# Variance of the gates in the PSUM bank, Newton's step for x on GpSimd

## What is computed

```python
x = x + conv_ref(ln_c(x), Wk, bk, Wq, bq, Wv, bv, Wr, br, heads=8)
#   k = relu(Wk x + bk), q = relu(Wq x + bq), v = Wv x + bv
#   context = k v^T per head (8 x 8), attended = context^T q, out = Wr attended + br
t = to_tokens(x)
t = t + ffn_ref(ln_t(t), router_w, router_b, expert_w, expert_b)
#   p = softmax(t router_w + router_b); the two best experts, their weights made to sum to 1
#   out = sum over the two of weight * (t expert_w[e] + expert_b[e])
x = from_tokens(t, x)
# both norms: (v - mean) / sqrt(var + eps) over the 64 channels, eps 1e-6 and 1e-5
```

## Time and profile before

| | |
|---|---|
| median of 3 runs | 662.58 us (661.94 to 663.03) |
| profiled execution, its time | 661.13 us |
| profiled execution, its span | 659.3 us |
| mean granted TensorE clock | 0.991 |
| busy: TensorE | 612.2 us (93%) |
| busy: VectorE | 506.5 us (77%) |
| busy: ScalarE | 420.3 us (64%) |
| busy: GpSimd | 396.4 us (60%) |
| chain that ended last, by engine | TensorE 72%, VectorE 18%, issue 6% |

### The profile page before, as it was taken

The page is one execution under the profiler, slowest core; times in us unless marked ns, Lnnn a source line. Parts: engine busy times, 40 slices in busy tenths (PEclk is TensorE's granted clock), DMA queues, the critical chain, the costliest instruction groups (busy, mean ns, idle before and its releaser), DMA issues.

```text
span 659.3 us, 21452 instructions
## 1 busy us (share of the span) xinstructions
PE 612.2 (93%) x8318; PEld 277.4 (42%) x8318; DVE 506.5 (77%) x1176; ACT 420.3 (64%) x800; POOL 396.4 (60%) x350
## 2 busy tenths in 40 slices
PE   3799989779999999999999999999999999999997
PEld 1566656444444444444444444444333333332232
DVE  3434444798888888898888888988798999989954
ACT  2265646576767676766676676775857667676552
POOL 7223252127666566667666566656677767777986
PEclk9999989799999999999999999999999999999999
DMA  6132535395555566655556665544565667545652
GB/s 151 33 100 67 146 100 130 81 226 132 139 131 138 141 158 160 145 134 127 145 129 147 146 162 129 129 120 109 133 150 135 145 159 176 130 96 120 151 132 49
DMA packets 32663, 86.22 MB, mean 131 GB/s; under 512 B 7650, under 2 KB 7826, under 8 KB 32562
## 3 DMA queue, kind: packets, MB, share of 16 engines
q1 hardware_dynamic: 32082, 84.64, 53.4%
q0 software_dynamic: 288, 0.19, 0.2%
q10 hardware_dynamic: 192, 0.01, 0.0%
HBM read 34.47 MB, written 16.78 MB: 78 GB/s over the span
## 4 chain that ended last, share of the span: by engine, by line
PE 72%; DVE 18%; issue 6%; ACT 2%; POOL 2%; DVEq 0%; ACTq 0%; POOLq 0%
PE bank L1103 28%; PE bank L1089 8%; PE bank L1026 6%; PE bank L1004 5%; PE bank L990 5%; DVE z L834 4%; PE bank L949 3%; PE bank L973 3%; PE bank L1050 3%; PE bank L1100 3%; DVE x L734 2%; DVE osb L844 2%; PE bank L1075 2%; DVE xnT L689 2%; DVE bank L749 1%
## 5 line engine op out<-in xcount | busy, mean ns | idle before, releaser
L442 POOL TENSOR_TENSOR z<-gbs,x1d 128x512 f32<-128x512 f32 x256 | 320.6, 1278 | 170.8 <-ACT gbs L579 78.0
L1106 PE MATMUL bank<-z,ew 128*64 128x512 f32 x512 | 244.6, 599 | 0.0
L1103 PE MATMUL bank<-z,ew 128*64 128x512 f32 x512 | 243.6, 598 | 0.0
L579 ACT COPY gbs<-bank 128x512 f32<-128x512 f32 x256 | 140.9, 595 | 46.4 <-PE bank L1089 46.0
L834 DVE TENSOR_TENSOR z<-bank,x1d 128x512 f32<-128x512 f32 x256 | 165.3, 678 | 6.3 <-PE bank L1089 6.3
L433 POOL TENSOR_TENSOR xsq<-xin 128x512 f32<-128x512 f32 x64 | 65.4, 1044 | 85.0 <-DMA xin<-in_x_dram 67.4
L1103 PEld LDWEIGHTS bank<-z,ew 128*64 128x64 f32 x512 | 64.9, 136 | 103.4 <-issue 96.9
L1089 PE MATMUL bank<-grows,sel 64*64 64x512 f16 x1024 | 85.7, 387 | 6.1 <-ACT grows L573 4.8
L503 ACT COPY xn<-bank 128x512 f32<-128x512 f32 x64 | 34.4, 590 | 62.4 <-PE bank L949 62.4
L1106 PEld LDWEIGHTS bank<-z,ew 128*64 128x64 f32 x512 | 64.4, 136 | 1.1 <-POOL z L442 1.1
L734 DVE SCALAR_TENSOR_TENSOR x<-bank,br_col,x_again 128x512 f32<-128x512 f32 x64 | 45.0, 745 | 20.0 <-PE bank L1050 20.0
(11 more groups left out here) (135 smaller groups left out, 819.9 us busy)
## 6 DMA issues: line engine op xcount, KB each, us to landing
x1d<-x SPq DMA_DIRECT2D x128, 256.0 KB, 4.5
xin<-in_x_dram SPq DMA_DIRECT2D x64, 256.0 KB, 4.2
x_again<-in_x_dram SPq DMA_DIRECT2D x64, 256.0 KB, 4.1
out_dram<-osb SPq DMA_DIRECT2D x128, 128.0 KB, 2.6
k<-in_const_dram SPq DMA_DIRECT2D x1, 453.5 KB, 4.0
ew_nat<-in_L_ffn_expert_w_dram POOLq DMA_DIRECT2D x2, 64.0 KB, 6.4
sel<-in_const_sel_dram SPq DMA_DIRECT2D x1, 128.0 KB, 3.3
bk_rows<-bk_wide ACTq DMA_DIRECT2D x6, 1.0 KB, 1.7
```

Source lines behind the costliest of these rows:

```text
L442: pool.tensor_tensor(z[:, 1, i % R_Z, :], gbs[:, i % R_Z, :], x1d[:, g % 2, 1, u * NT:(u + 1) * NT], ALU.mult).then_inc(z_pool, 1)
L579: nc.scalar.copy(gbs[:, i % R_Z, :], bank[:, :]).then_inc(taken_of(("spread", i, 1)), 1)
L1103: pe.matmul(out_bank[0:C, :], ew[:, j, :], z[:, 0, i % R_Z, :], start=False, stop=(j == PAIRS - 1), skip_group_check=True).then_inc(prod_d ...
L1106: pe.matmul(out_bank[C:P, :], ew[:, j, :], z[:, 1, i % R_Z, :], start=False, stop=(j == PAIRS - 1), skip_group_check=True).then_inc(prod_d ...
```

## The change

Two edits. In the gates the variance is kept in a third short row of bank 7 (`dev_work[2]`) and no longer in SBUF (`bstat[:, 1]`); the first of Newton's three products multiplies it with the root (one operand in PSUM, one in SBUF) where it multiplied the root with itself (both in SBUF), and the second multiplies that with the root. And Newton's step for x leaves VectorE: GpSimd makes it in four instructions of 128x16, `x_newton`, ahead of its products of slot 3; `normalise` and the next group's `x_deviations` wait for the new semaphore `xstat_pool`.

```diff
@@ sizes and banks
-        dev_work = [bank[7][:, QG * E + QG * i:QG * E + QG * (i + 1)] for i in range(2)]
+        dev_work = [bank[7][:, QG * E + QG * i:QG * E + QG * (i + 1)] for i in range(3)]
+        xstat_pool = sem("xstat_pool")
-        N_XSTAT, N_GATE = 7, 27
+        N_XSTAT, N_NEWTON, N_GATE = 4, 4, 27
@@ GpSimd
+            def x_newton(g):
+
+                own, root, work = g * N_NEWTON, xstat[:, 4, :], xstat[:, 5, :]
+                pool.wait_ge(xstat_root, g + 1)
+                pool.tensor_tensor(work, root, root, ALU.mult).then_inc(xstat_pool, 1)
+                pool.wait_ge(xstat_pool, own + 1)
+                pool.tensor_tensor(work, work, xstat[:, 2, :], ALU.mult).then_inc(xstat_pool, 1)
+                pool.wait_ge(xstat_pool, own + 2)
+                pool.tensor_scalar(work, work, -0.5, 1.5, ALU.mult, ALU.add).then_inc(xstat_pool, 1)
+                pool.wait_ge(xstat_pool, own + 3)
+                pool.tensor_tensor(rstd[:, g % 2].rearrange("p u a -> p (u a)"), work, root, ALU.mult
+                                   ).then_inc(xstat_pool, 1)
...
             for n in range(STEPS):
                 for k in range(SLOTS):
+                    if k == 3 and real(n - L_COLS):
+                        x_newton(n - L_COLS)
                     for i in iterations(n, k + 1):
                         product(i)
@@ VectorE, x_deviations and normalise
-                    lambda: dve.reciprocal(xstat[:, 3, :], xstat[:, 2, :]),
-                    *newton(rstd[:, g % 2].rearrange("p u a -> p (u a)"), xstat[:, 4, :], xstat[:, 2, :],
-                            (xstat[:, 5, :], xstat[:, 0, :]))]
+                    lambda: dve.reciprocal(xstat[:, 3, :], xstat[:, 2, :])]
...
-                    elif k == 4:
-                        dve.wait_ge(xstat_root, g + 1)
+                        upto(dve, xstat_pool, g * N_NEWTON)
...
-                dve.wait_ge(xstat_dve, (g + 1) * N_XSTAT)
+                dve.wait_ge(xstat_pool, (g + 1) * N_NEWTON)
@@ VectorE, gates
+                def gate_root():
+                    dve.wait_ge(dev_root, p + 1)
+                    return dve.scalar_tensor_tensor(dev_work[0], dev_work[2], -0.5, bstat[:, 3, :], ALU.mult, ALU.mult)
...
-                    lambda: dve.tensor_scalar(bstat[:, 1, :], dev_work[1], 0.0, EPS_FFN, ALU.max, ALU.add),
-                    lambda: dve.reciprocal(bstat[:, 2, :], bstat[:, 1, :]),
-                    rooted, dev[1], dev[2],
+                    lambda: dve.tensor_scalar(dev_work[2], dev_work[1], 0.0, EPS_FFN, ALU.max, ALU.add),
+                    lambda: dve.reciprocal(bstat[:, 2, :], dev_work[2]),
+                    gate_root,
+                    lambda: dve.tensor_tensor(dev_work[1], dev_work[0], bstat[:, 3, :], ALU.mult),
+                    lambda: dve.scalar_tensor_tensor(bstat[:, 0, :], dev_work[1], 1.5, bstat[:, 3, :],
+                                                     ALU.add, ALU.mult),
@@ VectorE, the loop over steps and slots
-                    if k == 3 and real(n - L_COLS):
-                        x_deviations(n - L_COLS, 4, N_XSTAT)
```

More of the change, by code:

```diff
@@ L651, in then @@
                     dve.wait_ge(set_dve, n_set[0])
[L653 to L657, removed]
             def halves(a):
@@ L749, in start @@
                     return dve.scalar_tensor_tensor(halves(dev_work[0]), mean, -1.0, mean, ALU.mult, ALU.mult)
-                def rooted():
-                    dve.wait_ge(dev_root, p + 1)
-                    return dev[0]()
                 def choose():
@@ L789, in total @@
                     return dve.tensor_scalar(second_work, gstat[:, 4, :], 1.0, None, ALU.add)
-                dev = newton(bstat[:, 0, :], bstat[:, 3, :], bstat[:, 1, :], dev_work)
                 steps = [
```

## The result

| | before | with the change |
|---|---|---|
| median of the runs | 662.26 us (660.6 to 663.03, 4 runs) | 654.08 us (650.39 to 654.75, 4 runs) |
| profiled execution, its time | 661.13 us | 654.75 us |
| profiled execution, its span | 659.3 us | 652.9 us |
| mean granted clock | 0.991 | 0.994 |

The ratio is 0.9868, with a 95% interval from 0.9827 to 0.991. The forecast was 652.8 us, a gain of 9.8. The medians differ by 8.2 us, the two profiled executions by 6.4.

What follows compares the result with a forecast made beforehand. TensorE was taken as the bound from 144 to 444 us, losing time only to VectorE's lateness. 7.75 + 1.9 + 0.15 = 9.8 us off the 662.58 us median gave 652.8 us, range 649.8 to 658.0.

Steps and rivals of the forecast that it cites:

- What bounds the kernel: From 144 to 444 us TensorE is the bound; VectorE's lateness for L834 costs it 1.55 us in one loaded step.
- Gates' variance in the bank: Gates' L655 falls to 0.20 us, but the stall moves to L767: gain 0.55 us of VectorE's time, not 0.97.
- The price of 0.065 us: 62 cycles more for a PSUM source, in two gates' instructions; by it the ramp gains 0.26 us less, sum 9.5.
- 0.55 and 1.52 us of VectorE's time: Loaded step: 0.55 from the gates' edit and 1.52 from Newton's step leaving VectorE bring L834 2.07 us earlier.
- The sum of the loaded steps: From 144 to 444 us the full 1.55 us comes back in five loaded steps: 7.75 us.
- The ramp, 1.9 us: From 115 to 146 us, Newton's step leaving three VectorE chains saves 0.5 + 0.9 + 0.5 = 1.9 us.
- Newton's step on GpSimd, 1.3 us, hidden: Four dependent 16-column instructions take 1.3 us, hidden from 144 us on where GpSimd idled 1.65 us between products.
- Rival A: L767 waits behind GpSimd's whole Newton chain, so 1.0 of each 1.55 us stays lost: 4.7 us gained, 657.9; chance 0.19.
- Before 115 us nothing: In early steps Newton's step has 1.91 us and uses 1.3, so TensorE neither gains nor loses.
- B: Newton's step on GpSimd late in eight early steps, losing 8 x (T - 1.9); at T = 3.6 us, 666.4; chance 0.06.
- C: Nothing measurable, within 1.3 us: another lateness, say ScalarE's exponential, replaces VectorE's at the same place; chance 0.08.
- D: More than the sum: the ramp's shorter wait for keys keeps the clock up, 2.6 us more, 650.2; chance 0.07.

Runs made afterwards that it cites:

- the mended order: GpSimd's ten set-up instructions for the experts' bias placed ahead of Newton's step in step 11, against the changed kernel: 653.68 us; again on another chip 652.55 us.
- both orders mended: Changed kernel with GpSimd's expert-bias set-up ahead of Newton's step in step 11 and VectorE's x variance in slot 1 behind the gates: 651.6 us, ratio 0.985.
- the kernels with more work: Changed kernel with GpSimd's four Newton instructions for x made two or three times over: 658.86 us (ratio 0.995) and 671.95 us (ratio 1.0152).
- the third group: Runs on one chip beside the kernel before (661.69 us): x's variance behind the gates 656.11, both repairs 651.6, expert-bias set-up ahead again 652.55 us.

## Why the prediction was right, and where its sizes were off

*What bounds the kernel.* Right: TensorE had one large wait for VectorE in five loaded steps, and without it the stretch from turn_x to the experts takes 2.72 us, as in the steps with a fold.

*Gates' variance in the bank.* Right in its mechanism: L792 takes 0.185 to 0.20 us everywhere, and the stall moved to L770 (0.70 us in place of 0.44), as forecast. The price of 0.065 us for an operand read from the bank did not show: the reciprocal of 128x32 takes 0.357 us from the bank and took 0.353 from SBUF, and L792 is no longer than an unstalled L655. Only the weight of the edits was misjudged: the prediction added 0.55 and 1.52 us of VectorE's time and did not price one alone. Its own numbers do that for x: 0.55 us later with 0.4 to spare is 0.15 lost in the stretch, and the run had 0.16. For the gates' edit alone they don't: it is enough too, since the second stall existed only because the first had pushed Newton's step under GpSimd's next product.

*The sum of the loaded steps, 5 x 1.55 = 7.75 us.* It measured 6.63, 1.33 for a pair. The step that failed is that the 1.55 of one stretch was carried to the whole step. VectorE, early now, meets GpSimd's other product at L677 (0.60 in place of 0.21 us), 0.22 us of which reaches TensorE. The prediction looked for who is late next as far as L689 in slot 0, and not into slot 1.

*The ramp, 1.9 us.* In the waits it was 1.5: 0.4 for the keys (3.9 to 3.5), 0.8 for L949 (1.3 to 0.5), 0.3 for L1036 (1.2 to 0.9), for 0.5 + 0.9 + 0.5. The step times gave 2.4. Of these 1.13 lie in the second step, at a granted clock of 1.00 in both kernels, where the waits for L949 and L1036 stand; the first step's 1.25 hold 0.4 of waits, and the clock was 0.75 before and 0.86 after. So what the forecast's own mechanism gave is 1.5; the rest is luck.

*Newton's step on GpSimd, 1.3 us, hidden.* It took 1.2 to 1.3 us, 0.20 to 0.22 us an instruction and 0.30 from start to start, and the loaded steps would have hidden three times as much. Rival A's condition did not come true: VectorE got its turn before Newton's chain, and GpSimd waited.

*Before 115 us nothing.* Wrong by 1.6 us in the profiled execution of the change, by 1.4 in the one beside the mended order (9.62 against 8.25 us). The prediction said of this queue that no DMA is issued from it in the loop and weighed the products behind Newton's step, but not the once-only set-up that stands behind it in step 11. It had even used its rows as a price. An instruction that waits for ScalarE was put ahead of ten that had no other engine to wait for.

*Total.* 9.8 us forecast; 6.4 between the profiled executions, the difference of 3.4 being 1.1 for L677, 1.6 for the set-up and 1.2 for the late start, less 0.5 that the ramp and the last loaded step gave beyond their 2.05. The medians gave 8.2 and, with more runs, 6.2. So the 654.08 us of the four runs came nearer to the forecast than the change deserves: the waits and steps that it moved give 6.6 + 0.35 in the loaded stage, 1.5 less 0.13 in the ramp and behind it, and cost 1.6, together 6.7 us. The rest of the 8.2 belongs to no wait that the change moved. With both orders mended it is 10.1.

*The rivals.* A fell as said. B's rule was confirmed in its size by the kernels with more work (1.74 against 1.7 us a step), and is far from T = 1.2. C fell: TensorE was the bound of the loaded steps once VectorE was early. D is real in size (the last section), but no run shows that this change brings it about.

## What to carry to other kernels

When a stall is removed, everything behind it moves earlier, against another part of the neighbour's work: follow the engine through the whole period, not just to the next consumer. When an instruction that waits is put into an in-order queue, list all that stands behind it, the once-only set-up among it, and put what waits for nobody ahead. And stalls in a row are not added up: remove one alone first, since the second may be its consequence.

## What the runs showed of the hardware that was not expected

A `TENSOR_SCALAR` of 128x16 with a single operand in SBUF stood still beside GpSimd's product as long as the form with two (0.60 us for 0.17). Small GpSimd instructions are cheap: 128x16 takes 0.20 to 0.22 us, less than the 0.23 and 0.30 of 1x64, and a dependent chain goes at 0.30 us an instruction.

The ramp's two steps (from the 12th to the 14th key bias after the first) depend on TensorE's granted clock by as much as on the change. Here they are in four executions, columns as above for TensorE alone; before:

```profile
117.30:145.60 28.30, 20.45 (x402) 0.88 0.60 149
```

the change:

```profile
120.10:146.10 26.00, 19.62 (x406) 0.93 0.65 155
```

the set-up's order alone, and the very same kernel in the third group, there with the step that follows:

```profile
118.61:145.58 26.97, 20.60 (x403) 0.87 0.63 150
...
117.50:142.10 24.60, 18.05 (x406) 1.00 0.69 165
142.10:162.20 20.10, 18.48 (x262) 1.00 0.57 130
```

One kernel took 27.0 us at 0.87 and 24.6 at 1.00, 2.4 us apart. But 1.8 of that went again in the next step, which took 20.1 us where it takes 18.3 in the other execution. TensorE stood still there for 1.6 us, in the middle of L1014, and the profile shows nothing that it waited for; the kernel with Newton's step twice has the same (1.9 us). Why is open. Of twelve profiled executions three had 1.00 in the ramp's two steps, all with Newton's step on GpSimd; with it on VectorE there were only two, at 0.88 and 0.94. Whether the shorter waits make the high clock likelier is open, since no kernel was profiled often enough. Such differences are a part of why the runs of one kernel spread over 3 to 7 us, but not shown to be the whole. Two kernels that differ by 1 us can't be told apart by whole times, but they can by their loaded steps, which repeat within 0.02 us; what such a change costs elsewhere, as in the ramp above, must then be looked for too.
